# A wavelet mixing layer on one core: ACT copies block 0 between the high and the low moves of the last edge

## What is computed

```
for _ in range(_LEVEL):            # 3 levels
    a, d = _dwt(a)
    details.append(d)
coeffs = [a] + details[::-1]
...
    enh.append(c * w[i])           # by channel
rec = enh[0]
for d in enh[1:]:
    rec = _idwt(rec[:, :d.shape[-1]], d)
...
return x + xr @ proj_w.T + proj_b
```

## Time and profile before

| | |
|---|---|
| median of three runs | 2392.61 us (2391.41 to 2397.37) |
| profiled execution, its own time | 2393.7 us |
| its span in the trace | 2391.8 us |
| granted TensorE clock, mean of the span | 0.997 |
| PE busy | 2340.1 us (98%) |
| PE weight loads busy | 2193.8 us (92%) |
| DVE busy | 1750.9 us (73%) |
| ACT busy | 1830.6 us (77%) |
| POOL busy | 290.7 us (12%) |
| HBM traffic | 434 MB, 182 GB/s over the span |

### The profile page before, as it was taken

The page is one execution under the profiler, slowest core; times in us unless marked ns, Lnnn a source line. Parts: engine busy times, 40 slices in busy tenths (PEclk is TensorE's granted clock), DMA queues, the critical chain, the costliest instruction groups (busy, mean ns, idle before and its releaser), DMA issues.

```text
span 2391.8 us, 85183 instructions
## 1 busy us (share of the span) xinstructions
PE 2340.1 (98%) x33948; PEld 2193.8 (92%) x33948; DVE 1750.9 (73%) x2906; ACT 1830.6 (77%) x3938; POOL 290.7 (12%) x1111
## 2 busy tenths in 40 slices
PE   6999999999999999999999999999999999999997
PEld 5999999999999999999999999999999999999996
DVE  3777777777777777777777777777777777777775
ACT  2877777777777777777777777777777777777776
POOL 2111111111111111111111111111111111111110
PEclk9999999999999999999999999999999999999999
DMA  3446454454545445464464544544454454644643
GB/s 125 160 160 238 160 204 185 170 200 180 190 185 204 167 179 213 160 239 160 160 238 160 207 183 169 200 179 186 185 207 163 179 217 160 239 160 160 238 161 120
DMA packets 106678, 439.38 MB, mean 184 GB/s; under 512 B 6785, under 2 KB 8065, under 8 KB 106370
## 3 DMA queue, kind: packets, MB, share of 16 engines
q1 hardware_dynamic: 105232, 434.13, 48.2%
q10 hardware_dynamic: 1138, 0.30, 0.1%
HBM read 217.33 MB, written 217.06 MB: 182 GB/s over the span
## 4 chain that ended last, share of the span: by engine, by line
PE 97%; issue 1%; DVE 1%; POOL 0%; ACTq 0%; ACT 0%; DMA 0%; DVEq 0%
PE proj_ps L392 30%; PE coefs_ps L342 30%; PE synth_ps L421 11%; PE synth_ps L433 10%; PE synth_ps L444 6%; PE synth_ps L435 3%; PE synth_ps L423 2%; PE proj_ps L402 2%; PE synth_ps L446 2%; POOL scale_sb L298 0%; ACTq L526 0%; DMA comp_sb<-comp_w 0%; DVE proj_lo L611 0%; DVE coefs_sb L604 0%; ACT stack_sb L567 0%
## 5 line engine op out<-in xcount | busy, mean ns | idle before, releaser
L342 PEld LDWEIGHTS coefs_ps<-analysis_sb,x_sb 64*128 64x128 f32 x13248 | 958.5, 188 | 116.9 <-DVE coefs_sb L604 61.4
L342 PE MATMUL coefs_ps<-analysis_sb,x_sb 64*128 64x84 f32 x13248 | 1020.7, 270 | 25.4 <-DVE coefs_sb L604 18.2
L392 PE MATMUL proj_ps<-w_sb,coefs_sb 64*128 64x64 f32 x13248 | 876.7, 271 | 1.9 <-issue 0.9
L611 DVE TENSOR_TENSOR proj_lo<-proj_ps,proj_hi 128x512 fp32r<-128x512 f32 x828 | 567.4, 686 | 375.4 <-ACT proj_hi L536 375.4
L392 PEld LDWEIGHTS proj_ps<-w_sb,coefs_sb 64*128 64x128 f32 x13248 | 820.6, 189 | 4.6 <-issue 3.8
L604 DVE TENSOR_TENSOR coefs_sb<-coefs_ps,scale_sb 128x552 f32<-128x552 f32 x828 | 604.3, 730 | 230.7 <-PE coefs_ps L342 215.5
L536 ACT ACTIVATE proj_hi<-proj_ps 128x512 fp32r<-128x512 f32 x828 | 471.9, 596 | 190.3 <-PE proj_ps L402 157.9
L554 ACT ACTIVATE stack_sb<-proj_hi 20x512 fp32r<-20x512 f32 x621 | 390.9, 630 | 207.0 <-DVE proj_lo L611 201.9
L631 DVE TENSOR_TENSOR x_sb<-synth_ps,x_sb 128x512 f32<-128x512 f32 x828 | 530.9, 682 | 20.8 <-PE synth_ps L446 14.4
L307 POOL TENSOR_TENSOR coefs_sb<-coefs_sb 128x20 f32<-128x20 f32 x828 | 187.1, 226 | 1915.9 <-DVE coefs_sb L604 1915.9
L554 ACT ACTIVATE stack_sb<-proj_lo 20x512 fp32r<-20x512 f32 x621 | 390.5, 629 | 15.2
(11 more groups left out here) (46 smaller groups left out, 2827.2 us busy)
## 6 DMA issues: line engine op xcount, KB each, us to landing
out<-x_sb SPq DMA_DIRECT2D x184, 1152.0 KB, 6.7
x_sb<-x SPq DMA_DIRECT2D x182, 1152.0 KB, 11.7
x_sb<-x SPq DMA_DIRECT2D x1, 1024.0 KB, 8.5
x_sb<-x SPq DMA_DIRECT2D x1, 768.0 KB, 6.0
x_sb<-x SPq DMA_DIRECT2D x1, 512.0 KB, 4.2
stack_sb<-bias_parts ACTq DMA_DIRECT2D x12, 2.0 KB, 1.7
edge_sb<-edge_m ACTq DMA_DIRECT2D x1, 128.0 KB, 6.1
synthesis_sb<-synthesis_m ACTq DMA_DIRECT2D x1, 64.0 KB, 6.1
```

The costliest lines, as they stand in the source:

```text
L342: return lambda cols: nc.tensor.matmul(coefs_ps[:, w // PART_WINDOWS, at:at + HALF_COLS], x_sb[half_rows[side], w, cols], analysis_sb[half ...
L392: mm = nc.tensor.matmul(out_cols[:, :, p, :], coefs_of(g, p)[rows, own_cols(w)], w_sb[rows, rows].rearrange("k (h c) -> k h c", h=2), star ...
L611: nc.vector.tensor_tensor(proj_lo[w][:, :].rearrange(by_node, n=2), proj_of(w)[:, :, 0:NODE_COLS], proj_hi[w][:, :].bitcast(fp32).rearrang ...
```

## The change

`move_tail` is split in two calls. Before, one call made the four moves of the high part and the four of the low part, and `copy_high` of window 0 followed. Now the call for the high part comes first, then `copy_high` of window 0, then the call for the low part, then `copy_high` of window 1. Each of the two calls has the waits on `tail_hi_copied` and on `synthesised` of its own.

```diff
-            def move_tail(turn, g, first):
+            def move_tail(turn, g, at, source, first):
                 group = turn * GROUPS + g
                 act.wait_ge(tail_hi_copied, group + 1)
                 if not (first and g == 0):
                     act.wait_ge(synthesised, group * 2 - 1)
-                for at, source in ((HIGH_AT, tail_hi), (LOW_AT, tail_lo)):
-                    if source is tail_lo:
-                        act.wait_ge(tail_lo_copied, group + 1)
-                    for q in range(4):
...
+                if at == LOW_AT:
+                    act.wait_ge(tail_lo_copied, group + 1)
+                for q in range(4):
...
-                    move_tail(turn, g, first)
+                    move_tail(turn, g, HIGH_AT, tail_hi, first)
                     copy_high(turn, g, 0, first)
+                    move_tail(turn, g, LOW_AT, tail_lo, first)
                     copy_high(turn, g, 1, first)
```

More of the change, by code:

```diff
@@ L561, in move_tail @@
                     act.wait_ge(synthesised, group * 2 - 1)
-                for at, source in ((HIGH_AT, tail_hi), (LOW_AT, tail_lo)):
-                    if source is tail_lo:
-                        act.wait_ge(tail_lo_copied, group + 1)
-                    for q in range(4):
[L566 to L569, removed]
+                if at == LOW_AT:
+                    act.wait_ge(tail_lo_copied, group + 1)
+                for q in range(4):
+                    cols = slice(q * PAIRS * QUAD, (q + 1) * PAIRS * QUAD)
+                    nc.scalar.activation(stack_sb[LATE][at:at + HALO_COLS, cols],
+                                         source[q * QUAD:q * QUAD + HALO_COLS, :].bitcast(fp32),
+                                         ACT.Copy).then_inc(tail_moved, 1)
             def turn_of(turn, first=False):
```

## The result

The changed kernel takes **2368.26 us**, the median of 4 runs (2366.0 to 2369.4), against 2394.85 for 4 runs of the kernel before (2391.4 to 2397.4). The ratio is 0.9889, with a 95% interval from 0.9872 to 0.9906. That is 26.6 us faster, where 19.7 were forecast. The profiled execution took 2369.4 us, with a span of 2367.6.

A forecast was written before the change was run, and what follows sets the result against it. PE was taken as the bound. 177 seams at 0.11 us gave 19.5 and turn 0 gave 0.2, together 19.7 us, taking the median 2392.6 to 2373 us; the forecast's own range was 2368 to 2377, the stated range 2369 to 2386.

The forecast's parts named there:

- What bounds the kernel: PE, 98% busy, sets the end; 0.11 us a group is lost to the path ACT copy, split, scaling, load.
- seam: On PE, last edge product to first projection matmul, between groups: 0.74 us, forecast to become 0.63.
- (a): ACT's copy of window 0 moves ahead of four low moves, ending at 1209.24 instead of 1210.57; DVE's split then fills idle time.
- (b): DVE's scaling of pair 3 waits for PE alone, starting 0.20 us earlier, worth only 0.11 on PE.
- unit price: Gain on PE per group between matmuls: 0.11 us, with rounding 0.10 to 0.12.
- its twin: The same instructions on PE half a group earlier, unhindered: 0.63 us from last edge product to first projection matmul.
- (c): ACT's low moves end at 1210.57 instead of 1209.95; PE's wait for them is taken as hidden, cost zero.
- the doubt about the slack: PE's wait for the low moves has 0.62 us slack at the edge products' load, or 0.09 if taken at line 433.
- price for a lost cover: If PE's wait for the low moves is no longer hidden, each 0.1 us costs about 20 us in all.
- slower than before: Rival, chance 0.03: three waits before ACT's low moves cost 0.08 each, PE stands 0.15 in 205 groups: 2404 us.
- (d): ACT's pair of window copies is broken, 2 x 0.60 instead of 1.09, ACT 0.13 us longer, hidden by 0.5 us slack.
- The sum: Of 205 places, 177 give 0.11 us, 8 in turn 0 give 0.03, 20 behind the loop's branch nothing: 19.7 us.

## Why the prediction was wrong, point by point

**What bounds the kernel: right.** PE sets the end, and the seam's path was ACT copy, split, scaling, load. The order of waits after the change, and above all the kernel with the copy one move earlier, show it.

**(a) and (b), the copy and the scaling: right.** DVE's wait for ACT at line 611 fell by 276 us (about 270 forecast), its scaling of pair 3 now waits 1.15 us for PE (about 1.0 forecast), the load of the seam starts 0.02 behind the last edge product (0.03 forecast), and the 20 us of seams are there: 0.11 a group in the median and 0.10 in the mean. In time the pair of kernels with the load earlier puts the whole change at 16.8 us without the branch. The unit price of 0.11 is thus right to about 0.02. The seam did not stop at the 0.63 of the forecast, and its twin went to 0.605 as well; both come from measuring at the last edge product, which starts about 0.02 later behind the one beside it after the change. What moves it there was not tried.

**(c), the low moves: right that they are hidden, and the doubt about the slack is settled.** The waits cost nothing, and PE takes its wait for the moves with the edge products. The slack there is 0.67 by the prediction's own numbers and not 0.62, which changes nothing else. Its price for a lost cover, 20 us for each 0.1, was too high: 0.18 of idle load cost about 0.03 between matmuls. With both copies ahead of the moves the edge load idles 0.18 us (29.0 / 158). The rival "slower than before" was not near: even that kernel is 19 us faster than before.

**(d), the broken pair: nearly right.** Line 536 rose from 471.9 to 489.7 us of busy time, less than the 0.11 x 207 = 23 of two full copies for a pair: the copy behind the high moves takes 0.57 in the rows and not 0.60, and it starts 0.09 before their end. The forecast assumed that moves and copies never overlap. It cost nothing, as forecast. The Trainium skill, in ScalarE: Activation LUTs, section What ACT_TABLE_LOAD costs, has back-to-back ACTIVATEs overlap by about 93 ns. The trace agrees in size (0.09) for a copy behind the high moves, and not for copies behind or ahead of the low moves, where it shows a gap of 0.02 to 0.03. What the prediction makes of that page, low moves that end 0.3 us earlier, is also too little: from the last high move to the last low one there are five joints, and at each 0.093 of overlap in place of a gap of 0.02 would give over 0.5 us (an estimate). Measurement decides here: the overlap has a condition.

**The sum: this is the step that failed.** It said that 20 seams "lie behind the loop's branch and give nothing". The seam behind the branch indeed gave nothing, but the pause at the branch was taken as a constant, 15.2 us in 20 waits before and after. Of the waits that it shows, this was the only one that did not name an engine, and the prediction used it as a boundary of the count without asking what it was waiting for. The runs show that it fell to 7.7 us, and the sum of the pauses by 7.5, which is the size of the 7 us between 19.7 and 26.6. The range inherited the error: the rounding of the seam's price alone gave 2368 to 2375, the forecast's own range began at 2368, and the range as stated began at 2369; the measured 2368.3 lies just below that. A bound for this row, from nothing to all of its 15.2 us, would have been the honest one.

**What makes PE pause.** Shown: with the load's traffic gone from the stretch, the long pauses are gone, in both kernels; with the load moved to another stretch, the fetch there begins some 2.5 us later and PE stalls. Shown too: the change shortens the pauses by way of the seams in the groups ahead, not by ACT's order at the branch. **Open:** how free seams make PE ask for its last fetch earlier. With the load out of the way, that fetch starts 3.8 to 4.5 us ahead of the last analysis load in the kernel before, and 4.0 to 4.4 in some turns and 5.2 to 5.8 in others in the changed one; so PE does seem to run through its instructions in another phase. No run here took that apart, and nothing tried here controls it.

**The best version** is the changed order with the load of that slot ahead of the store: 2362.95 us, 31 us or 1.3% below the kernel before and 4 to 5 us below the change alone. The ranges of single runs do not overlap (2360.3 to 2363.8, and 2365.4 to 2368.7), but they are of different sessions, and the intervals of the two ratios overlap (0.9853 to 0.9888, and 0.9872 to 0.9906).

## What to carry to other kernels

Look for work on a helper engine whose input is ready while it stands in line behind work that nobody needs yet; and price the exchange by the distance between the bound engine's own instructions, since of a wait of 1.35 us on DVE only about 0.20 mattered, and only 0.11 of those on PE. Never leave an "issue" wait of the bound engine as a constant in the sum: it is a resource too, here its instruction fetch beside a large load, and both a new schedule and the place of a DMA can move it. Where a loop's branch shows such a pause, try the load that runs there earlier; later may put it where it hurts more.

## What the runs showed of the hardware

- **PE's instruction fetch and a large load get in each other's way.** With the DMA engines 90 to 100% busy ahead of the branch PE paused 0.76 to 1.26 us; with the same place at 0.00 it took 0.23 to 0.33. A load placed behind the branch cost some 2 us a turn, and the fetch there began 3.1 to 3.8 us after the hint in place of 0.6 to 1.2. Moving one load of 2.3 MB per turn was worth 14 us (0.6%) where it came 14 us earlier, and cost 84 us (3.5%), with the clock's part in it, where it came 11 us later.
- **An ACT instruction starts before the one ahead has ended only in some pairs.** Behind moves that write from row 0 a copy that writes from row 0 starts 0.09 early; behind moves that write from row 32 it starts 0.02 late, and so do moves at row 32 behind a copy (0.03). Exchanging the moves exchanged the overlap. The Trainium skill gives such a rule for VectorE alone, in VectorE: DVE Perf Modes, section Two Vector instructions with no wait between them: an instruction is held where its output starts in another quadrant of partitions than the last output into the same memory, or an input in another quadrant than the first input of the last instruction that read that memory. ACT's rows here fit that rule. Its second half is needed for the high moves that start 0.02 behind copy 0 in the kernel with the low moves first: they write from row 0 as the copy did, but read `tail_hi` from row 0 where the last read of that memory, by a low move, was from row 96. That the rule holds for ACT in general is not shown.
- **Idle time of the weight loads is not the same time lost between matmuls.** The load's idle time of 0.27 was 0.11 in the distance between matmuls at the seam, and one of 0.18 was about 0.03 at the edge products. The loads run ahead: at the free seam the load starts at 1189.27 and its matmul at 1189.44.
